# A change of order: three 1 MB weight loads leave GpSimd later in attention, and the product with the last inverse sums stands later in the output projection

## The chip, the cores and the metric

One core of a Trainium2 chip runs the whole program. The metric is the device time of one execution in microseconds (us). Three runs of the kernel before took 865.54, 867.91 and 869.71 us; the median is 867.91 us. Engines are named as in the profile: PE (TensorE's matmuls) and PEld (its weight loads), DVE (VectorE), ACT (ScalarE), POOL (GpSimd), SP (SyncE, which here only issues DMAs).

## What is computed

```python
x = x + attn(layernorm(x), qkv_w, qkv_b, proj_w, proj_b)      # x is 4 x 1024 x 256 f32
x = x + experts(layernorm(x), centroids, ln_g, ln_b, w1, b1, w2, b2)
```

Attention has 16 heads of 16 columns, rotary positions and a causal mask; its output goes through a 256 x 256 projection. Each of the 4096 tokens is then given to the one of 8 experts whose centroid has the largest product with it. The expert normalises the token, multiplies it by w1 (256 x 1024), applies relu and multiplies by w2 (1024 x 256). The result is weighted with a sigmoid of that product.

## The kernel before, in words

The kernel has three stages. Each engine has a program of its own, written out by hand; semaphores join them, and a wait holds up everything behind it on its engine.

**Projection** (to about 130 us of the span): layer norm, q, k and v. The rotated q and k are split into bf16 parts and stored to a DRAM tensor `qk_parts`.

**Attention** (about 130 to 523 us) works on 16 items Q, each being four heads of one batch; NQ is 16. An engine's `emit(i)` is one step. In step i PE computes the scores and the weighted sums of item i (`scores`, line 1252; `pv`, line 1269) and the maxima that item i+1 needs (`put_item`, line 1156). PE's first maxima product of a new item waits until that item's 14 stack transfers have landed (line 1135). ACT takes exponentials (line 929), DVE reduces block maxima (line 1009), POOL masks the diagonal blocks (line 843).

SP's order in step n (lines 735 to 757) is:

1. `store_inverse(n-3)`: wait for the reciprocals, store 16 KB (line 228).
2. `place_out(n-2)`: four transfers of 64 KB (line 213) and four of 4 KB (line 217).
3. Wait for `nm`, which POOL writes at the start of the step (lines 829 to 834), and load it in two transfers (line 744).
4. `spread_inverse(n-3)`: one transfer (line 235) that writes 4 DRAM rows of 4 KB to 64 partitions, 16 copies of each: 256 KB. Its source is broadcast as 4 x 16 x 1024.
5. `load(n+2)`: wait for PE, then the 14 stack transfers of 64 or 128 KB from `qk_parts` (lines 387 to 401).
6. In steps 5, 7 and 9, three stores of a padding row block (line 757).

POOL's order in step i: at k = 1 it writes `nm` (its first instruction is line 829, once per step); at k = 4 it issues the second weights of an expert if `early_at` names this step:

```python
        early_at = (1, 2, 3, 4, 5, 14)
        W2_AT = 4
```

Expert e's second weights (1 MB, 128 partitions of 8 KB) go to the arena columns from e times W2C. The first six experts are loaded here (LOADED is 6), and the earliest reader is the first expert product in the last stage. Even steps from 4 also hold POOL's product with the inverse sums (line 242, at k = 10). The places of the other operations are fixed by k too.

**Output projection, routing and experts** (523 us to the end). The first part has 16 pairs u of 128-token tiles. PE projects a pair (line 2053) once the addition two pairs back is done; DVE's `add(u)` (line 1673) adds the residual. Between the additions DVE has the routing: `one_hot`, `positions`, `row_scalars`, and at u = 8 `first_table`, whose end (line 1770) sets `s_tab` to 2, which names the expert and the rows of the first eight slots. POOL scatters token rows to DRAM (line 1506) group by group. The attention output of the last two items still has to be multiplied by their inverse sums; DVE does it in `normalize_out(dve, 7)`, a 128 x 1024 product (line 242) ahead of routing work, and it sets `s_nm` to 8. Who waits for that: PE before pair 12 (line 2037), and SP before it loads the second weights of expert 6 (line 1459), since the inverse sums lie in their place.

SP's order there, which is one queue: the residual rows, `col` and `b2r`, expert 6's second weights (after `s_nm`), expert 7's, then after `s_tab` the first weights of slot 0 (`load_w1`, line 246, 1 MB), then after the first four groups' scatters have landed the rows of slots 0 and 1 (line 344), then the first weights of slot 1. ACT normalises slot 0's rows (line 1557), PE turns them (line 1996) ahead of its last pair, and the experts' loop starts.

Of the kernel before, what the change touches and what calls it, by code (L numbers as in the profile page):

```python
# [130 lines left out]
def program(nc, x, x_feat, w_qkv, b_qk, b_val, w_proj, w_proj_out, b_proj, cent, w_exp, cols, b2, consts, rope, out):  # L131
    ctx = ExitStack()
    with ctx:
# [191 lines left out]
        with nc.sbuf_tensor("q_stack", [P, RS, 2, GH * SEQ], BF16) as qs, \  # L325
                nc.sbuf_tensor("k_stack", [P, RS, 2, GH * SEQ], BF16) as ks:
            s_stk = [sem(f"stack_loaded{i}") for i in range(RS)]
            s_fix = sem("fixed_rows_preset")

            phase_project_attend(nc, x, x_feat, w_qkv, b_qk, consts, rope, parts_d, w_exp, s_w, arena, v_all, spare, cst, ident, eps,  # L330
                                 qs, ks, s_fix, s_stk, s_st, s_cst, started, ones3, load_first, value_bias, add_value_bias,
                                 s_bw, load_bias_rows, split_bias, w_proj_out, ctc, xl, s_cc, centroid_means, centre_centroids, bias_columns, keep_bias_columns, bias_logits,
                                 keep_bias_logits, weight_logits, keep_weight_logits, pay_d, s_pad0, s_pad,
                                 o_late, s_vq, s_oe, s_oc, s_dc, place_out, invert_sums, store_inverse, spread_inverse, normalize_out)
# [72 lines left out]
def phase_project_attend(nc, x, x_feat, w_qkv, b_qk, consts, rope, parts_d, w_exp, s_w, arena, v_all, spare, cst, ident, eps,  # L407
# [5 lines left out]
    with ExitStack() as ctx:  # L413
# [238 lines left out]
        def wait_free(eng, i, item, alone=None):  # L652
            wait(eng, s_free, i, ITEMS, number(i, item) + 1, alone)

        early_at = (1, 2, 3, 4, 5, 14)
        W2_AT = 4
        assert len(early_at) == LOADED
        BY_POOL = NQ // 2 - 2
# [630 lines left out]
def phase_route_experts(nc, x, pay_d, load_w1, load_rows, load_half_rows, row_data, row_scalar, wait_rows, w2s, w1b, s_w1, cols, b2, cst, ident, eps, slot_tab, col, b2r,  # L1289
# [3 lines left out]
    with ExitStack() as ctx:  # L1293
# [134 lines left out]
        def expert_of(eng, S, known):  # L1428

            if S.reg is not None:  # L1430
                return expert(eng, S)
            if S.const not in known:
                known[S.const] = expert(eng, S)
            return known[S.const]
# [5 lines left out]
        with nc.Block() as block:  # L1440
# [210 lines left out]
            def _(dve):  # L1651
# [15 lines left out]
                def add(u):  # L1667
                    n, at = 2 * u + 1, 2 * u % R
                    two = xr[:, n - 1:n + 1, 0:DIM]
                    dve.wait_ge(s_pj, n + 1)  # L1670
                    last = 2 * n // G >= len(s_x) - 1
                    dve.wait_ge(s_x[-1] if last else s_x[2 * n // G], 32 if last else 16)
                    dve.tensor_tensor(two, ps_p[:, at:at + 2, 0:DIM], two, ALU.add).then_inc(s_x2, 1)
                    dve.tensor_tensor(xl[:, n - 1:n + 1, :], ps_p[:, at:at + 2, DIM:DIM + NE], xl[:, n - 1:n + 1, :],
                                      ALU.add).then_inc(s_lg, 1)

                def stats(u):
                    before = 2 * pairs_by(False, u)
                    dve.wait_ge(s_x2, u + 1)
                    if before >= R:  # L1680
                        dve.wait_ge(s_v, before + 2 - R)
                    for i in range(2):
                        dve.bn_stats(st[:, (before + i) % R, :], xr[:, 2 * u + i, 0:DIM]).then_inc(s_bn, 1)
                    for i in range(2):
                        dve.wait_ge(s_bn, before + i + 1)
                        dve.bn_aggr(mv[:, 2 * u + i, :], st[:, (before + i) % R, :]).then_inc(s_v, 1)

                def one_hot(g):
                    r, k = g % 2, GROUPS[g]
                    riota = cst[:, C_RIOTA:C_RIOTA + NE].unsqueeze(1).to_broadcast([P, k, NE])  # L1690

                    def over_experts(ap):
                        return ap.unsqueeze(2).to_broadcast([P, k, NE])

                    dve.wait_ge(s_lg, starts[g + 1] // 2)
                    dve.tensor_reduce(top[:, of(g)], xl[:, of(g), :], AX.X, ALU.max).then_inc(s_tp, 1)
                    dve.wait_ge(s_tp, 4 * g + 1)
                    dve.tensor_tensor(ge[:, 0:k, :], xl[:, of(g), :], over_experts(top[:, of(g)]), ALU.is_ge).then_inc(s_tp, 1)
                    dve.wait_ge(s_tp, 4 * g + 2)
                    dve.tensor_tensor(pick[:, 0:k, :], ge[:, 0:k, :], riota, ALU.mult).then_inc(s_tp, 1)  # L1700
                    dve.wait_ge(s_tp, 4 * g + 3)
                    dve.tensor_reduce(pm[:, 0:k], pick[:, 0:k, :], AX.X, ALU.max).then_inc(s_tp, 1)
                    dve.wait_ge(s_tp, 4 * g + 4)
                    if g >= 2:
                        dve.wait_ge(s_rk, g - 1)
                    dve.tensor_tensor(hot[:, r, 0:k, :], riota, over_experts(pm[:, 0:k]), ALU.is_equal).then_inc(s_hot, 1)

                def positions(g):
                    r, k = g % 2, GROUPS[g]
                    dve.wait_ge(s_rk, g + 1)  # L1710
                    dve.wait_ge(s_sn, g)
                    dve.tensor_tensor(rank[:, 0:k, :], ps_k[:, 0:k, :], seen[:, :].unsqueeze(1).to_broadcast([P, k, NE]),
                                      ALU.add).then_inc(s_rc, 1)
                    dve.wait_ge(s_rc, 3 * g + 1)
                    dve.tensor_tensor(seen[:, :], ps_k[:, G, :], seen[:, :], ALU.add).then_inc(s_sn, 1)
                    dve.tensor_tensor(mine[:, 0:k, :], rank[:, 0:k, :], hot[:, r, 0:k, :], ALU.mult).then_inc(s_rc, 1)
                    dve.wait_ge(s_rc, 3 * g + 2)
                    dve.tensor_reduce(posf[:, 0:k], mine[:, 0:k, :], AX.X, ALU.add).then_inc(s_rc, 1)
                    dve.wait_ge(s_rc, 3 * g + 3)
                    dve.tensor_copy(posi[:, of(g)], posf[:, 0:k]).then_inc(s_ps, 1)  # L1720

                def row_scalars(g):
                    dve.wait_ge(s_sd, 2 * (g + 1))
                    dve.reciprocal(sd[:, 2, of(g)], sd[:, 0, of(g)]).then_inc(s_rs, 1)
                    dve.reciprocal(xr[:, of(g), COL_S], sd[:, 1, of(g)]).then_inc(s_sb, 1)
                    dve.wait_ge(s_rs, g + 1)
                    dve.tensor_tensor(xr[:, of(g), COL_K], sd[:, 1, of(g)], sd[:, 2, of(g)], ALU.mult).then_inc(s_sb, 1)
                    dve.tensor_tensor(xr[:, of(g), COL_GATE], top[:, of(g)], sd[:, 2, of(g)], ALU.mult).then_inc(s_sb, 1)
                    dve.wait_ge(s_sb, 4 * g + 1)
                    dve.scalar_tensor_tensor(out=xr[:, of(g), COL_B], in0=mv[:, of(g), 0], scalar=-1.0, in1=xr[:, of(g), COL_S],  # L1730
                                             op0=ALU.mult, op1=ALU.mult).then_inc(s_sb, 1)
# [112 lines left out]
                for u in range(NP):  # L1844
                    add(u)
                    if u == 2:
                        invert_sums(dve, NQ - 1)
                    if u == 7:
                        normalize_out(dve, NQ // 2 - 1)
                    if u % 2 == 0 and 2 <= u <= 2 * FIRST_GROUPS:  # L1850
                        positions(u // 2 - 1)
                        row_scalars(u // 2 - 1)
                    if u % 2 == 1 and u < 2 * FIRST_GROUPS:
                        one_hot(u // 2)
                    if u < 2 * FIRST_GROUPS and u not in BY_ACT:
                        stats(u)
                    if u == 2 * FIRST_GROUPS:
                        first_table()
                    if u > 2 * FIRST_GROUPS:
                        stats(u - 1)  # L1860
                    if u == starts[FIRST_GROUPS + 1] // 2:
                        one_hot(FIRST_GROUPS)
                    if u in (2 * FIRST_GROUPS + 2, 2 * FIRST_GROUPS + 4):
                        dve.wait_ge(s_tab, 2)
                        expert_of(dve, Step(u // 2 - FIRST_GROUPS - 1), known)
                    if u == starts[FIRST_GROUPS + 1] // 2 + 2:
                        positions(FIRST_GROUPS)
                        row_scalars(FIRST_GROUPS)
                    if u == starts[FIRST_GROUPS + 2] // 2:
                        one_hot(FIRST_GROUPS + 1)  # L1870
# [310 lines left out]
```

## Time and profile before

| | |
|---|---|
| median of three runs | 867.91 us (865.54 to 869.71) |
| the profiled execution, own time | 862.7 us |
| its span in the profile | 861.0 us |
| mean granted clock of TensorE | 0.98 |
| PE busy in the span | 805.0 us (93%) |
| DVE, ACT, POOL busy | 594.6, 517.0, 340.4 us |

The profile shows one execution. A time in a row is counted from the start of the span. A row of the timeline names the start, the busy time, the engine, the line, the operation, the result and its inputs, and in brackets how long the engine sat idle before it and what ended that. The word "issue" there means that the engine waited for nothing that the profile shows.

### The profile page before, as it was taken

The page shows a single profiled execution, that of the slowest core. Times are in us where ns is not written, and L with a number is a line of the kernel's source. Part 1 is how long each engine was busy: PE and PEld are TensorE (multiplying, and loading weights), DVE is VectorE, ACT ScalarE, POOL GpSimd, SP SyncE. Part 2 cuts the span into 40 slices and gives each one's busy share as a digit, 9 for nine tenths or more (in the row PEclk, how much of TensorE's full clock was granted, in tenths as well). Part 3 has the DMA queues.
Part 4 walks back from the last instruction along what each step waited for, and adds up shares of the span by engine and source line. Part 5 has one row for each costly group of instructions (what it writes and reads, how often), then busy time and mean ns, then how long its engine had stood idle before and what let it go on. Part 6 is the DMA issues. An engine that isn't in the chain of part 4 may idle for free. (4 is left out here: it accounts for less than half of the span.)

```text
span 861.0 us, 24382 instructions
## 1 busy us (share of the span) xinstructions
PE 805.0 (93%) x8788; PEld 494.0 (57%) x8789; DVE 594.6 (69%) x1145; ACT 517.0 (60%) x1211; POOL 340.4 (40%) x476
## 2 busy tenths in 40 slices
PE   6999868999998999999999988877999999999994
PEld 4555433444343444443444434566999999999873
DVE  5878999999898999999999704764733333333353
ACT  4668335888787888888888894223333333333351
POOL 9999672443242434334343432634111111143211
PEclk9999988999999999999999999899999999999998
DMA  8578632445447343343334315866555555556550
GB/s 289 165 240 252 200 111 76 132 126 112 120 99 163 95 115 102 86 109 84 82 90 97 76 43 174 273 218 206 182 185 185 182 182 180 183 191 194 178 207 4
DMA packets 63354, 128.90 MB, mean 150 GB/s; under 512 B 16981, under 2 KB 44246, under 8 KB 56982
## 3 DMA queue, kind: packets, MB, share of 16 engines
q1 hardware_dynamic: 59094, 112.53, 44.5%
q0 software_dynamic: 4160, 15.03, 5.3%
q8 instruction: 64, 1.05, 0.5%
q14 instruction: 36, 0.29, 0.1%
HBM read 99.89 MB, written 22.98 MB: 143 GB/s over the span
## 5 line engine op out<-in xcount | busy, mean ns | idle before, releaser
L929 ACT ACTIVATE arena<-ps_pair 128x512 f32<-128x512 f32 (+2 forms) x640 | 317.9, 557 | 64.6 <-PE ps_pair L1252 61.8
L1009 DVE TENSOR_REDUCE B_block_max<-ps_item 128x8 f32<-128x1024 f32 x288 | 335.4, 1217 | 28.2 <-PE ps_item L1156 27.8
L1252 PE MATMUL ps_pair<-q_stack,k_stack 99*32 99x512 bf16 (+7 forms) x3072 | 197.5, 331 | 2.7 <-ACT arena L929 1.8
L843 POOL TENSOR_SCALAR_AFFINE_SELECT arena<-arena 128x256 f32<-128x256 f32 x256 | 102.1, 408 | 153.3 <-ACT arena L929 151.2
L1269 PE MATMUL ps_pair<-arena,B_v_quad 128*32 128x512 f32 (+3 forms) x1536 | 155.9, 487 | 1.2 <-ACT B_oacc L948 0.7
L1252 PEld LDWEIGHTS ps_pair<-q_stack,k_stack 99*32 99x32 bf16 (+1 forms) x3072 | 69.0, 95 | 119.7 <-ACT arena L929 60.8
L2099 PE MATMUL C_ps_p<-arena 128*128 x512 | 118.0, 382 | 4.4 <-issue 4.4
L2075 PEld LDWEIGHTS C_bank<-arena 128*128 128x128 f32 x1024 | 120.3, 193 | 2.5 <-ACT arena L1595 0.6
L2075 PE MATMUL C_bank<-arena 128*128 128x128 f32 x1024 | 120.7, 277 | 0.4 <-ACT arena L1625 0.4
L1156 PE MATMUL ps_item<-k_stack,q_stack 64*128 64x128 bf16 (+2 forms) x1280 | 107.3, 265 | 14.7 <-DVE B_block_max L1009 8.9
L1625 ACT ACTIVATE arena<-C_bank,ffn_columns 128x128 f32<-128x128 f32 x128 | 36.5, 367 | 121.9 <-PE C_bank L2075 109.8
L2099 PEld LDWEIGHTS C_ps_p<-arena 128*128 128x128 f32 x512 | 95.2, 191 | 17.6 <-issue 6.0
L1532 POOL DMA_INDIRECT out<-C_res,C_ids x32 | 31.8, 993 | 180.6 <-issue 125.8
L1156 PEld LDWEIGHTS ps_item<-k_stack,q_stack 64*128 64x128 bf16 x1280 | 45.5, 94 | 86.5 <-DVE B_block_max L1009 43.9
L1926 DVE TENSOR_SCALAR arena<-C_bank,ffn_columns 128x128 f32<-128x128 f32 x128 | 36.0, 345 | 79.0 <-PE C_bank L2075 67.2
L1269 PEld LDWEIGHTS ps_pair<-arena,B_v_quad 128*32 128x32 f32 x1536 | 42.5, 109 | 28.5 <-issue 11.5
L1196 PE MATMUL ps_pair<-arena 128*128 128x512 f32 x128 | 58.3, 598 | 0.0
L780 POOL TENSOR_TENSOR arena<-arena 128x512 f32<-128x512 f32 x32 | 51.1, 1608 | 5.6 <-DVE arena L1050 5.2
L1595 ACT ACTIVATE arena<-C_bank,ffn_columns 128x128 f32<-128x128 f32 (+1 forms) x78 | 30.8, 445 | 35.4 <-PE C_bank L1996 34.5
L1906 DVE TENSOR_TENSOR C_y<-C_ps_p,ffn_bias 128x256 f32<-128x256 f32 x32 | 13.6, 424 | 52.7 <-PE C_ps_p L2099 52.6
L1050 DVE SCALAR_TENSOR_TENSOR arena<-ps_pair,A_bq,arena 128x512 f32<-128x512 f32 x64 | 44.5, 742 | 7.6 <-PE ps_pair L1196 7.5
L1506 POOL DMA_INDIRECT payload<-C_x_rows,C_posi x32 | 31.5, 986 | 41.8 <-issue 29.3
(213 smaller groups left out, 781.0 us busy)
## 6 DMA issues: line engine op xcount, KB each, us to landing
arena<-in_w_exp SPq DMA_DIRECT2D x41, 1024.0 KB
qk_parts<-arena SPq DMA_DIRECT2D x32, 384.0 KB, 3.5
q_stack<-qk_parts SPq DMA_DIRECT2D x96, 128.0 KB, 3.5
k_stack<-qk_parts SPq DMA_DIRECT2D x64, 128.0 KB, 3.5
arena<-in_w_exp POOLq DMA_DIRECT2D x6, 1024.0 KB, 7.0
rows<-payload SPq DMA_DIRECT2D x32, 130.5 KB, 2.1
arena<-in_x SPq DMA_DIRECT2D x8, 512.0 KB, 4.7
arena<-in_x_feat SPq DMA_DIRECT2D x8, 512.0 KB, 5.6
```

The source lines that it names most:

```text
L780: pool.tensor_tensor(rot[:, h % 2, c, :], rot[:, h % 2, c, :], ds[:, h % 2, 1 - c, :], op).then_inc(s_rot, 1)
L843: pool.affine_select(out=block_p, in_=block_p, compare_op=ALU.is_ge, fill=0.0, base=0, pattern=[[0, 2], [1, P]], channel_multiplier=-1).th ...
L929: act.activation(pr[s % PR][:, h:h + 2 * n - 1:2, 0:W], ps_s[(EXPS * Q.const + exps_to[s] + u) % R][:, 0:n * W].rearrange("p (h n) -> p h ...
L1009: dve.tensor_reduce(bmx[:, g:QH:GH, first:first + 3 * gap + 1:gap], src[:, :, :].rearrange("p c (b n) -> p c b n", n=P), AX.X, ALU.max).th ...
L1050: dve.scalar_tensor_tensor(out=out[:, h % 2, at, :], in0=ps_qk[h % 2][:, c, :], scalar=bq[:, n:n + 1], in1=rp[:, table, positions(h)], op0 ...
L1156: mm = pe.matmul(dst[:, half, at * P:(at + n) * P], qs[rows, r, half, bass.ds(g * SEQ + t * P, P)], ks[rows, r, half, bass.ds(g * SEQ + kb ...
L1196: mm = pe.matmul(ps_qk[h % 2][:, c, :], wq[:, k, at:at + P], z[:, g % 2, k, :], start=(k == 0), stop=(k == DC - 1))
L1252: mm = pe.matmul(bank[at:at + 32, :], ks[rows, r, half, bass.ds(g * SEQ + kb * P + at, 32)], qs[rows, r, half, bass.ds(g * SEQ + c * QW + ...
L1269: mm = pe.matmul(ps_o[32 * h:32 * h + 32, off:QW], vq[:, r, kb, h, :], pr[s % PR][:, h, 0:QW - off], start=(kb == 0), stop=(kb == 4 * c + ...
L1625: act.activation(hr[:, S.ring(2), c, :], ps_h[0][:, c, :], ACT.Relu, bias=col[:, bass.ds(e, 1), 2 * DC + c]).then_inc(s_r[0], 1)
L2075: mm = pe.matmul(ps_h[f // HC][:, f % HC, :], w1b[:, S.ring(W1R), at:at + P], xT[:, r, c, :], start=(c == 0), stop=(c == DC - 1))
L2099: mm = pe.matmul(ps_y[r], hr[:, r, c, :], w2s[:, bass.ds(e * W2C + c * DIM, DIM)], start=(c == 0), stop=(c == FC - 1))
```

## The change

Two constants are changed. The list of steps in which the second weights are issued has 4, 6 and 8 where it had 3, 4 and 5, for experts 2, 3 and 4. The product with the last inverse sums stands behind `add(9)`, the tenth addition, where it stood behind `add(7)`; `positions(3)`, `row_scalars(3)` and `first_table` of u = 8 now stand ahead of it. No work is added or taken away.

```diff
-        early_at = (1, 2, 3, 4, 5, 14)
+        early_at = (1, 2, 4, 6, 8, 14)
...
                     add(u)
                     if u == 2:
                         invert_sums(dve, NQ - 1)
-                    if u == 7:
+                    if u == 9:
                         normalize_out(dve, NQ // 2 - 1)
```

## Rows read from the trace of the kernel before

**Rows 1.** The page: busy time of each engine in us, share of the span, instructions.

```profile
PE 805.0 (93%) x8788; PEld 494.0 (57%) x8789; DVE 594.6 (69%) x1145; ACT 517.0 (60%) x1211; POOL 340.4 (40%) x476
```

**Rows 2.** Timeline of POOL: the cast at the start of steps 3, 4, 5, 6 and 8.

```profile
199.21 0.29 POOL L829 CAST B_n<-B_nr 96x128 bf16<-96x128 f32 x1 [6.16 <-DVE B_nr L1004]
...
226.04 0.29 POOL L829 CAST B_n<-B_nr 96x128 bf16<-96x128 f32 x1 [8.32 <-DVE B_nr L1004]
...
249.94 0.29 POOL L829 CAST B_n<-B_nr 96x128 bf16<-96x128 f32 x1 [4.33 <-DVE B_nr L1004]
...
277.66 0.29 POOL L829 CAST B_n<-B_nr 96x128 bf16<-96x128 f32 x1 [8.48 <-DVE B_nr L1004]
...
325.46 0.29 POOL L829 CAST B_n<-B_nr 96x128 bf16<-96x128 f32 x1 [6.66 <-DVE B_nr L1004]
```

**Rows 3.** Timeline of all engines in steps 3 and 5: where PE stood.

```profile
215.09 0.11 PEld L1269 LDWEIGHTS ps_pair<-arena,B_v_quad 128*32 128x32 f32 x2 [1.16 <-issue]
...
222.57 0.61 PE L1156 MATMUL ps_item<-k_stack,q_stack 64*128 64x512 bf16 x4 [1.74 <-DMA k_stack<-qk_parts]
...
266.16 0.20 PEld L1156 LDWEIGHTS ps_item<-k_stack,q_stack 64*128 64x128 bf16 x6 [2.01 <-issue]
...
274.20 0.60 PE L1156 MATMUL ps_item<-k_stack,q_stack 64*128 64x512 bf16 x4 [1.94 <-DMA k_stack<-qk_parts]
```

**Rows 4.** Line 824, the weight loads: steps 3 to 5, step 4 alone, step 14 alone.

```profile
L824 POOL DMA_DIRECT2D arena<-in_w_exp x3: 591/591/593, 205.6 to 256.3; - x3
DMA to landing us min/median/max: 6.8/11.9/12.8
...
DMA to landing us min/median/max: 6.8/6.8/6.8
...
L824 POOL DMA_DIRECT2D arena<-in_w_exp x1: 591/591/591, 475.3 to 475.3; - x1
DMA to landing us min/median/max: 7.2/7.2/7.2
```

**Rows 5.** Timeline of SP's queue: the spread of the inverse sums in steps 3, 4, 5, 8, 14.

```profile
204.45 0.61 SPq L235 DMA_DIRECT2D arena<-inverse_sums  x1
...
229.52 0.59 SPq L235 DMA_DIRECT2D arena<-inverse_sums  x1
...
255.37 0.60 SPq L235 DMA_DIRECT2D arena<-inverse_sums  x1
...
330.71 0.59 SPq L235 DMA_DIRECT2D arena<-inverse_sums  x1
...
473.06 0.60 SPq L235 DMA_DIRECT2D arena<-inverse_sums  x1
```

**Rows 6.** Windows (steps 6, 7, 8, weights later): engines busy, PEclk, DMA share, GB/s.

```profile
281.66:283.66 2.00, 2.00 (x32) 0.66 (x26) 2.00 (x2) 1.64 (x4) 0.77 (x2) 1.00 0.21 59
...
311.56:313.56 2.00, 2.00 (x48) 1.22 (x44) 1.69 (x3) 1.55 (x4) 0.64 (x2) 1.00 0.81 172
...
335.46:337.46 2.00, 2.00 (x48) 1.22 (x44) 1.69 (x3) 1.55 (x4) 0.65 (x2) 1.00 0.67 195
...
553.00:566.00 13.00, 12.65 (x65) 8.69 (x66) 11.14 (x54) 1.09 (x6) 5.80 (x7) 1.00 0.91 321
```

**Rows 7.** Timeline of DVE, SP and ACT around the last product, 550 to 570 us.

```profile
550.95 1.22 DVE L242 TENSOR_TENSOR arena<-arena 128x1024 f32<-128x1024 f32 x1
...
557.29 0.67 DVE L1673 TENSOR_TENSOR C_x_rows<-C_ps_p,C_x_rows 128x512 f32<-128x512 f32 x1
...
552.20 0.80 SPq L1460 DMA_DIRECT2D arena<-in_w_exp  x2
...
558.89 0.01 SPq L246 DMA_DIRECT2D arena<-in_w_exp  x1
...
566.95 1.44 SPq L344 DMA_DIRECT2D rows<-payload  x2
...
569.05 0.60 ACT L1557 ACTIVATE arena<-rows 128x256 f32<-128x256 f32 x1 [5.01 <-DMA rows<-payload]
```

## The prediction

> **What bounds the kernel now.** I read the page first: PE is busy for 805.0 us of the span [rows 1], so a time in which PE stands still is nearly all lost. Next I looked for places where it stands. POOL's cast at the start of each attention step serves as a clock [rows 2]. From step 3 to step 4 it takes 226.04 - 199.21 = 26.83 us, from 4 to 5 23.90, from 5 to 6 27.72, and from step 6 to step 8 47.80, which is twice 23.90. So 23.90 us is an undisturbed step, and two of them are longer: step 3 by 2.93 us and step 5 by 3.82, together 6.75. The timeline says where [rows 3]. In step 3 PE's weight loads have a gap of 1.16 us that ends with "issue", and later PE waits 1.74 us for the stack of the next item: 2.90 together. In step 5 it is 2.01 and 1.94, together 3.95. The second kind is plain: the 14 stack transfers landed late. The first kind names nothing. I take it for the fetch of PE's instructions, held up on the same DMA engines; the row does not prove that.
>
> What do these two steps have? The weight loads issued in steps 3 to 5 landed 11.9, 6.8 and 12.8 us after issue, by the median, the minimum and the maximum of the three and the row of step 4 alone: 11.9 and 12.8 are steps 3 and 5 [rows 4]. Step 4 holds the same 1 MB load and the same 14 stack transfers and loses nothing. The load is therefore not enough; its neighbour on the queues matters. SP's spread of the inverse sums is issued at 204.45, 229.52 and 255.37 in these steps [rows 5]. The weight load follows the cast by 6.4 us (205.6 - 199.21 and 256.3 - 249.94 [rows 2, 4]). So the spread runs ahead of the weight load by 1.1 us in step 3, 2.9 in step 4 and 0.9 in step 5, and in step 14 by 475.3 - 473.06 = 2.2, where the load lands after 7.2 us [rows 4, 5]. The closer the spread is, the later the weight load lands.
>
> **Part one: steps 3, 4, 5 become 4, 6, 8.** The removals first. Steps 3 and 5 no longer hold a weight load. Steps 6 and 7 hold none now and take 23.90 us each, though step 7 has the three stores too [rows 2]. So both should fall to 23.90: a gain of 6.75 us. POOL's issue itself (0.59 us [rows 4]) leaves one step for another, and POOL is busy for 40% of the span [rows 1]: it costs nothing in either place. The first reader of experts 2 to 4 stands behind the whole of attention, so landing later costs nothing.
>
> The additions are steps 6 and 8; step 4 keeps a load, of another expert. Step 4 must not be priced at zero because it was clean. It was clean because PE stood 1.74 us for the stack late in step 3, when SP had already begun the next step's round, so SP was early against POOL. That stall goes. The spread of step 4 then comes about 2.9 - 1.7 = 1.2 us ahead of the weight load instead of 2.9. Step 6 loses its early start in the same way. Step 8 needs no such reasoning: its spread already stands 330.71 - 325.46 = 5.25 us behind the cast and thus 1.1 us ahead of where the weight load will be issued [rows 2, 5], exactly as in step 3. I therefore expect three crowded steps in place of two.
>
> What holds them up? While the spread has the DMA engines nearly to itself their mean share is only 0.21 [rows 6], as if few of the 16 worked on it, and a transfer has landed only when the last engine is done. The Trainium skill (DMA: Bandwidth & Descriptors, Rules for kernel authors) says that a broadcast with a leading dimension of c copies confines a DMA to at most c engines; here c is 4, a share of at most 0.25, and the trace agrees with 0.21. A weight load that meets the spread would wait on those four engines, which is why I trust the spacing more than the parity of the step.
>
> The price of one crowded step lies between 0 (step 4 now) and 3.82 us (step 5). The "issue" part was 1.16 and 2.01: I take the mean, 1.6. The stack part was 1.74 and 1.94, but in odd steps. Even steps carry their stack transfers more easily: in windows of the same kind the DMA share is 0.81 at 172 GB/s in step 7 and 0.67 at 195 GB/s in step 8 [rows 6], so the backlog should be mostly gone before the stack is needed. I take 0.4. Three steps at 2.0 make 6.0, against 6.75 lost now: part one gains 0.7 us. Its ends are a gain of 6.75 (all three like step 4 now) and a loss of 3 x 3.82 - 6.75 = 4.7.
>
> The Trainium skill (Runtime: NRT & Kernel Launch, Instruction fetch mechanics) says that the fetch of the next instruction block is mostly hidden. By that rule the "issue" part would not come back, the three steps would cost 3 x 0.4 = 1.2 and part one would gain 5.5. The gaps of 1.16 and 2.01 us in the two steps that also have late DMAs [rows 3] speak against it here.
>
> **Part two: the product behind the tenth addition.** It takes DVE 1.22 us [rows 7]. Ahead of it now come the routing of u = 8 and the first slot table, so these finish about 1.0 us earlier: the tenth addition, at 557.29 now, moves to about 556.3. What lies behind it on DVE is late by no more than 0.3. PE waits for the product only before pair 12 and has work until then, so this costs 0. POOL's scatters need the row scalars, but POOL still has an earlier group to scatter then; the gain there is 0.
>
> The cost is on SP. Its loads of experts 6 and 7 wait for this product: they go out at 552.20 now, right behind its end at 552.17, and will at 556.3 + 0.85 (the addition's two instructions) + 1.22 = 558.4. Everything behind them on SP moves too. The first weights of slot 0, at 558.89 now, follow the pair by the 0.80 us of its issue and an estimated 1.5 for reading the slot's expert: about 560.7. The rows of slot 0 are issued at 566.95, when the scatters have landed, and ACT waited 5.01 us for them until 569.05 [rows 7]. They stand third in one queue behind 3 MB of weights. Those 3 MB start 6.2 us later than the first 2 of them do now. From 553 to 566 the weights and the scatters together moved 321 GB/s [rows 6]. At that rate 3.1 million bytes take 9.8 us; with an estimated microsecond from issue to first data they end at 569.2, and about 570 with what is left of the scatters. The rows then land at about 571 instead of 569. Pair 15 and the first expert product follow the rows on PE, so I count +2.0 us. Its bounds: 0, if the weights have drained by 567, and 6.2, the whole shift.
>
> **The sum.** -0.7 + 2.0 = +1.3 us. The profiled execution took 862.7 us, 5.2 below the median of 867.91; both changes are differences, so I add the sum to the median: 869.2 us.
>
> **The rivals.**
> 1. *The crowding does not come back.* If the trouble in steps 3 and 5 was that of odd steps, 4, 6 and 8 stay at 23.90 us. For: all lost time is in odd steps, and even ones have the lighter traffic. Against: step 14 is even and its load is slower than step 4's, with nothing else new but the spacing. Part one gives -6.75; with part two at +2.0 or 0 the time is 863.2 or 861.2. Chance 0.27.
> 2. *Three full losses: slower.* The place is PE in steps 4, 6 and 8, the mechanism the same as in step 5, and it decides from about 2.9 us a step. With 3.4 us each (the mean of steps 3 and 5), 10.1 - 6.75 + 2.0 = +5.4: 873.3. For: step 8's spacing equals step 3's. Against: the lighter stack traffic. Chance 0.17.
> 3. *The fetch is hidden, the stack part stays.* -5.5 + 2.0 = -3.5: 864.4. Against: the "issue" gaps. Chance 0.08.
> 4. *My forecast*: chance 0.48.
>
> That the change does not do what it says can be set aside: both are constants that place instructions.
>
> **How the numbers follow.** A measurement of this kernel can tell about 0.5%, 4.3 us, from no change. Faster than 863.6 holds most of rival 1, a third of rival 3 and a little of my own case: 0.26. Slower than 872.2 holds most of rival 2 and the part of my own case in which part two nears its upper bound: 0.21. The rest is 0.53. The range runs from 861.7, inside rival 1, to 873.5, just over rival 2.
>
> **What the profile after would show.** Right: POOL's cast intervals of steps 3 and 5 at 23.90; those of 4, 6 and 8 at 25 to 27, with an "issue" gap on PE in each; weight loads of steps 4, 6 and 8 landing after 9 to 12 us; the spread about 1.1 us ahead of each. The pair of loads at line 1460 issued at about 558 on the clock of before, and ACT's wait at line 1557 longer by 2. Wrong: landings near 7 us in steps 6 and 8 (rival 1), or rows of slot 0 landing no later.

## The result, and the profile after

| | before | after |
|---|---|---|
| median of six runs | 866.82 us (865.54 to 869.71) | 872.63 us (871.06 to 875.45) |
| span of the profiled execution | 861.0 us | 869.4 us |

The ratio is 1.0061, with a 95% interval of 1.0036 to 1.0087: slower, by about 5.3 us. The forecast was 869.2 us, which is 1.3 over the median of three runs, 867.91; the range went to 873.5. The measured time lies inside the range, near its upper end, and the loss is about four times the forecast one. The size is that of rival 2, three full losses; the single losses are made up differently, as the rows below show. The profiled execution of the kernel before took 862.7 us, less than each of its six runs, so its trace shows less trouble than its median run has.

The page of the kernel after, first block, beside [rows 1]:

```profile
PE 808.5 (93%) x8788; PEld 495.2 (57%) x8789; DVE 597.3 (69%) x1145; ACT 517.7 (60%) x1211; POOL 338.9 (39%) x476
```

PE does the same 8788 matmuls. Its idle time has grown from 56.0 us to 60.9 (869.4 - 808.5), and its busy time by 3.5. From the cast of step 1 to that of step 15 alone, PE's busy time grew by 2.3 us (335.13 to 337.46) for the same 5392 matmuls, which needs a reason of its own (below). The timeline of POOL shows which steps grew longer; it is the clock of [rows 2], here from step 4 on:

```profile
224.16 0.29 POOL L829 CAST B_n<-B_nr 96x128 bf16<-96x128 f32 x1 [6.65 <-DVE B_nr L1004]
252.51 0.29 POOL L829 CAST B_n<-B_nr 96x128 bf16<-96x128 f32 x1 [5.85 <-DVE B_nr L1004]
276.40 0.29 POOL L829 CAST B_n<-B_nr 96x128 bf16<-96x128 f32 x1 [6.65 <-DVE B_nr L1004]
303.14 0.29 POOL L829 CAST B_n<-B_nr 96x128 bf16<-96x128 f32 x1 [5.13 <-DVE B_nr L1004]
327.04 0.29 POOL L829 CAST B_n<-B_nr 96x128 bf16<-96x128 f32 x1 [6.65 <-DVE B_nr L1004]
356.04 0.29 POOL L829 CAST B_n<-B_nr 96x128 bf16<-96x128 f32 x1 [9.42 <-DVE B_nr L1004]
```

Step 4 takes 28.35 us, step 6 26.74 and step 8 29.00; steps 5 and 7 take 23.9. Over 23.90 that is 4.45, 2.84 and 5.10, together 12.4, where [rows 2] had 6.75. From the cast of step 1 to that of step 15 the kernel before took 341.41 us and the kernel after 347.20: 5.8 us more. From the cast of step 15 to the end it is 369.77 against 368.22, 1.55 more. The remaining 1.06 us of the 8.4 between the two spans lie ahead of step 1, where nothing was changed.

Where PE stood, from the timeline of PE in steps 4, 6 and 8, beside [rows 3]:

```profile
241.44 0.24 PE L1252 MATMUL ps_pair<-q_stack,k_stack 128*32 128x128 bf16 x3 [2.52 <-issue]
...
292.36 0.23 PE L1156 MATMUL ps_item<-k_stack,q_stack 64*128 64x128 bf16 x2 [1.89 <-issue]
...
299.68 0.61 PE L1156 MATMUL ps_item<-k_stack,q_stack 64*128 64x512 bf16 x4 [0.93 <-DMA k_stack<-qk_parts]
...
351.18 0.61 PE L1156 MATMUL ps_item<-k_stack,q_stack 64*128 64x512 bf16 x4 [3.74 <-DMA k_stack<-qk_parts]
```

These are the two kinds of gap of [rows 3], in another mixture in each step: step 4 has only the gap with "issue", step 8 only the wait for the stack, step 6 both. The gaps of steps 4 and 8 do not fill their losses: 2.52 of 4.45 and 3.74 of 5.10 us. The windows right behind them tell what else there is (the kernel after, columns as in [rows 6]):

```profile
238.90:241.40 2.50, 0.02 (x1) 0.00 (x0) 1.77 (x2) 0.19 (x1) 0.59 (x2) 1.00 1.03 198
241.40:244.00 2.60, 2.56 (x35) 0.90 (x35) 0.33 (x1) 1.26 (x3) 1.03 (x3) 0.81 1.03 203
244.00:248.00 4.00, 4.00 (x56) 1.55 (x52) 2.77 (x3) 2.59 (x5) 2.66 (x2) 0.70 0.38 83
...
351.20:353.00 1.80, 1.80 (x20) 0.52 (x24) 1.38 (x2) 0.83 (x2) 0.00 (x0) 0.79 0.48 78
353.00:356.00 3.00, 3.00 (x23) 0.66 (x15) 1.60 (x3) 1.49 (x4) 0.00 (x0) 0.56 0.03 4
```

PE is busy again, but part of the time at the lower of its two clock levels (1.2 in place of 2.4 GHz). In step 4 that loses 2.6 x 0.19 + 4 x 0.30 = 1.7 us, in step 8 1.8 x 0.21 + 3 x 0.44 = 1.7 us. With it the gaps account for the losses: 2.52 + 1.7 = 4.2 of 4.45 us in step 4, 1.89 + 0.93 = 2.8 of 2.84 in step 6, and 3.74 + 1.7 = 5.4 in step 8, which is 5.10 over and its successor 0.19. Behind the stack wait of step 5 before, which was 1.94 us, the clock stayed at 1.00:

```profile
274.20:276.00 1.80, 1.80 (x20) 0.58 (x24) 1.37 (x2) 0.81 (x2) 0.00 (x0) 1.00 0.67 117
```

The weight loads of these three steps (line 824) and the spread ahead of each (line 235, timeline of SP), beside [rows 4, 5]:

```profile
L824 POOL DMA_DIRECT2D arena<-in_w_exp x1: 593/593/593, 230.5 to 230.5; - x1
DMA to landing us min/median/max: 11.3/11.3/11.3
...
L824 POOL DMA_DIRECT2D arena<-in_w_exp x1: 593/593/593, 282.8 to 282.8; - x1
DMA to landing us min/median/max: 11.5/11.5/11.5
...
L824 POOL DMA_DIRECT2D arena<-in_w_exp x1: 593/593/593, 333.4 to 333.4; - x1
DMA to landing us min/median/max: 11.5/11.5/11.5
```

```profile
229.72 0.59 SPq L235 DMA_DIRECT2D arena<-inverse_sums  x1
...
281.48 0.59 SPq L235 DMA_DIRECT2D arena<-inverse_sums  x1
...
332.46 0.59 SPq L235 DMA_DIRECT2D arena<-inverse_sums  x1
```

The spread is 0.8, 1.3 and 0.95 us ahead. The place of the trouble and its neighbours on the queues came as the prediction had them, and the landings within its 9 to 12 us. Its size did not: the prediction had these steps at 25 to 27 us and an "issue" gap in each, and step 8 has none.

The second part of the change, from the timelines of DVE, SP and ACT, beside [rows 7]:

```profile
564.80 1.22 DVE L242 TENSOR_TENSOR arena<-arena 128x1024 f32<-128x1024 f32 x1
...
566.05 1.84 SPq L1460 DMA_DIRECT2D arena<-in_w_exp  x2
...
574.68 1.44 SPq L344 DMA_DIRECT2D rows<-payload  x2
...
577.76 1.09 ACT L1557 ACTIVATE arena<-rows 128x256 f32<-128x256 f32 x2 [3.71 <-DMA rows<-payload]
```

Counted from the cast of step 15 (499.63 here, 492.78 before), the loads of experts 6 and 7 leave SP at 66.4 in place of 59.4 us, and ACT has the rows of slot 0 at 78.1 in place of 76.3, 1.9 us later. Half of that is the rows' own issue, which the prediction held fixed: it comes at 75.1 in place of 74.2. From issue to ACT's start it is 3.1 us in place of 2.1. The first expert product on PE follows at 83.6 in place of 83.0.

### The profile page after: what moved, and what is told of

It reads as the page before. It is cut to its first block and busy times, and to the rows that moved or that the text cites. A ratio compares the mean times of both kernels' runs of the same rounds, so it can differ in the third digit from the quotient of the medians.

```text
span 869.4 us, 24382 instructions
## 1 busy us (share of the span) xinstructions
PE 808.5 (93%) x8788; PEld 495.2 (57%) x8789; DVE 597.3 (69%) x1145; ACT 517.7 (60%) x1211; POOL 338.9 (39%) x476
## 3 DMA queue, kind: packets, MB, share of 16 engines
q8 instruction: 64, 1.05, 0.5%
## 5 line engine op out<-in xcount | busy, mean ns | idle before, releaser
L2099 PE MATMUL C_ps_p<-arena 128*128 x512 | 119.8, 384 | 3.2 <-issue 2.9
L780 POOL TENSOR_TENSOR arena<-arena 128x512 f32<-128x512 f32 x32 | 49.1, 1546 | 4.4 <-DVE arena L1050 4.0
```

Of the source, the lines that this page charges most:

```text
L780: pool.tensor_tensor(rot[:, h % 2, c, :], rot[:, h % 2, c, :], ds[:, h % 2, 1 - c, :], op).then_inc(s_rot, 1)
L2099: mm = pe.matmul(ps_y[r], hr[:, r, c, :], w2s[:, bass.ds(e * W2C + c * DIM, DIM)], start=(c == 0), stop=(c == FC - 1))
```

## The experiments

None of the twelve kernels leaves out work. Each ratio is to the kernel before, run beside it on the same chip. k is the place within POOL's step at which the load is issued. "Lost" is the time from the cast of step 1 to that of step 15 in the one profiled execution, less 14 x 23.90 us; by this count the kernel before lost 6.8 and the kernel after 12.6. It comes from one execution, and the ratio from the medians.

| kernel | weights in steps, k | spread | lost | ratio (95%) |
|---|---|---|---|---|
| weights only | 1, 2, 4, 6, 8, 14; k = 4 | narrow | 18.2 | 1.0071 (1.0047 to 1.0095) |
| product only | as before | narrow | 7.4 | 1.0009 (0.9992 to 1.0027) |
| wide spread | as before | wide | 1.1 | 0.9908 (0.9883 to 0.9934) |
| moved, wide | 1, 2, 4, 6, 8, 14; k = 4 | wide | 0.2 | 0.9911 (0.9881 to 0.9941) |
| four narrow pieces | as before | narrow x4 | 9.7 | 0.9998 (0.9980 to 1.0017) |
| late | 1, 2, 14, 14, 15, 15 | narrow | 0.1 | 0.9898 (0.9873 to 0.9923) |
| late and wide | 1, 2, 14, 14, 15, 15 | wide | 0.1 | 0.9910 (0.9885 to 0.9935) |
| k = 6 | 1, 2, 4, 6, 8, 14; k = 6 | narrow | 10.7 | 1.0022 (0.9996 to 1.0049) |
| k = 2 | 1, 2, 4, 6, 8, 14; k = 2 | narrow | 0.4 | 0.9911 (0.9884 to 0.9938) |
| spread last | 1, 2, 4, 6, 8, 14; k = 4 | narrow, last | 2.4 | 0.9926 (0.9898 to 0.9955) |
| whole change, k = 2 | 1, 2, 4, 6, 8, 14; k = 2 | narrow | 0.0 | 0.9919 (0.9891 to 0.9947) |
| k = 2 again | 1, 2, 4, 6, 8, 14; k = 2 | narrow | 0.0 | 0.9903 (0.9873 to 0.9934) |

**1. The weight loads alone.**

```diff
-        early_at = (1, 2, 3, 4, 5, 14)
+        early_at = (1, 2, 4, 6, 8, 14)
```

> Half of the change: the list of steps is (1, 2, 4, 6, 8, 14), the product stays behind the eighth addition. In the trace of the changed kernel the cast intervals of steps 4, 6 and 8 are 28.35, 26.74 and 29.00 us (4.45, 2.84 and 5.10 over 23.90), together 12.4 us against the 6.75 that steps 3 and 5 lost before. Theory A (the loss is the crowding of the weight load and the spread in each step that has both close together): the same three intervals again, 26.5 to 29, steps 3, 5 and 7 at 23.9; the time 4 to 6 us over the kernel before. Rival B (the loss has to do with the moved product, or was chance in one execution): steps 4, 6 and 8 at 24 to 25 and the time within 1 us of the kernel before.

Measured: 862.20 us (858.23 to 866.75) against 856.12, which is +6.1. Steps 4, 6 and 8 took 31.35, 28.90 and 28.89 us; the landings were 14.0, 12.0 and 11.3 us, with the spread 0.5, 1.65 and 1.05 ahead. Theory A holds; step 4 and the time came out above its upper ends, 29 us and +6. The profiled execution was the slowest of the nine runs (866.75), so 18.2 us lost is more than the median run has. The PE waits of attention (the table of waits: total, times, longest):

```profile
PE ps_item L1156 <- DMA k_stack<-qk_parts: 8.5, 4, 3.5
PE ps_pair L1252 <- issue: 2.6, 1, 2.6
PE ps_item L1156 <- issue: 2.1, 1, 2.1
```

The stack is 8.5 of it, in even steps. So the parity of the step protects nothing.

**2. The product alone.**

```diff
-                    if u == 7:
+                    if u == 9:
                         normalize_out(dve, NQ // 2 - 1)
```

> The other half: the weight loads stay in steps (1, 2, 3, 4, 5, 14), the product goes behind the tenth addition. By the prediction's second part the loads of experts 6 and 7 leave SP about 6.2 us later, the rows of slot 0 land 2 us later and the kernel takes 2.0 us more (bounds 0 to 6.2). In the two traces the stretch from the cast of step 15 to the end is 369.77 us against 368.22, so 1.5 us more. Theory A: +1 to +2.5 us, and ACT's wait for the rows of slot 0 ends 1.5 to 3 us later counted from the cast of step 15. Rival: the later rows only eat waiting that exists anyway behind them, 0 to +0.5 us. Attention: steps 3 and 5 at 26.8 and 27.7 us as in the kernel before.

Measured: 856.73 us against 856.12, +0.8 us by the ratio, -0.7 to +2.3. Counted from the cast of step 15, SP's pair of loads went at 61.5 us, 5.0 later than in experiment 1, which has the product in its old place; ACT had the rows at 74.6 against 74.3. The first link of the prediction's chain is there, but here the rows came only 0.3 us later. That speaks for the rival; the time, with its interval, allows both. The loss in attention is that of the kernel before, 7.4 us, so what the change loses there comes from experiment 1.

**3. The wide spread.**

```diff
-            sp.dma_start(inv_all[half:half + HALF, :],
-                         inv_d[Q].unsqueeze(1).to_broadcast([QH, HD, SEQ])).then_inc(s_rb, 16)
+            for h in range(QH):
+                sp.dma_start(inv_all[half + h * HD:half + (h + 1) * HD, :],
+                             inv_d[Q][h:h + 1, :].to_broadcast([HD, SEQ])).then_inc(s_rb, 16)
...
-            eng.wait_ge(s_rb, 32 * (pair + 1))
+            eng.wait_ge(s_rb, 128 * (pair + 1))
```

> The kernel before with the spread of the inverse sums issued as four transfers, one for each head, whose leading dimension is the 16 copies and no longer the 4 heads. The same bytes go to the same places. Theory A (the spread sits on about four of the 16 DMA engines, and a weight load that meets it there lands late and holds up the stack and PE): the DMA share right behind the spread rises from 0.21 to over 0.5, the weight loads of steps 3 and 5 land in 7 to 9 us in place of 11.9 and 12.8, the intervals of steps 3 and 5 fall from 26.8 and 27.7 to 24 to 25, and the time falls by 3 to 6.5 us, less whatever SP's 1.8 us of further issue time in each step costs. Rival B (the whole load on the DMA engines, not its placing on few of them, sets the loss): the loads still land after 11 to 13 us, steps 3 and 5 stay at 26.5 to 28, the time is the same or up to 2 us longer.

Measured: 848.05 us against 856.12, -7.9 us (-10.0 to -5.7), more than the 3 to 6.5 expected. The weight loads of steps 3 to 5 landed after 5.5, 6.3 and 6.5 us. The casts of steps 3 to 6, timeline of POOL (its line is 830 here):

```profile
199.02 0.29 POOL L830 CAST B_n<-B_nr 96x128 bf16<-96x128 f32 x1 [6.15 <-DVE B_nr L1005]
222.91 0.29 POOL L830 CAST B_n<-B_nr 96x128 bf16<-96x128 f32 x1 [6.65 <-DVE B_nr L1005]
247.34 0.29 POOL L830 CAST B_n<-B_nr 96x128 bf16<-96x128 f32 x1 [4.34 <-DVE B_nr L1005]
271.76 0.29 POOL L830 CAST B_n<-B_nr 96x128 bf16<-96x128 f32 x1 [6.66 <-DVE B_nr L1005]
```

Step 3 takes 23.89 us; steps 4 and 5 take 24.43 and 24.42. The windows right behind the spread of steps 6 and 8, columns as in [rows 6]:

```profile
277.60:279.60 2.00, 2.00 (x50) 0.96 (x42) 1.59 (x3) 1.35 (x4) 0.82 (x2) 1.00 0.65 131
...
325.50:327.50 2.00, 2.00 (x50) 0.93 (x45) 1.59 (x3) 1.35 (x4) 0.90 (x3) 1.00 0.57 137
```

The DMA share is 0.65 and 0.57, where it was 0.21 [rows 6], for the same 256 KB. The Trainium skill (DMA: Bandwidth & Descriptors, Rules for kernel authors) ties the number of engines to the outermost dimension, and copies in front are its example. The prediction took c for the copies; here the 4 in front are the heads, and the 16 copies stand behind them. The trace agrees with the rule, with 4 in front at 0.21 and 16 in front at 0.6. Theory A holds.

**4. The change's list with the wide spread**: the edits of experiments 1 and 3 together.

> The change's list of steps (1, 2, 4, 6, 8, 14) together with the spread in four transfers of 16 leading copies, as in the run before it with that spread. There steps 3 and 5 fell to 23.89 and 24.42 us and the weight loads landed after 5.5 to 6.5 us. Theory A (the change loses because the narrow spread is close ahead of three weight loads): the intervals of steps 4, 6 and 8 at 23.9 to 24.5 us instead of 31.35, 28.90 and 28.89, landings of 5.5 to 7, time 6 to 9 us under the kernel before. Rival B (the wide spread only helped in odd steps): steps 4, 6, 8 above 26 us.

Measured: 848.55 us against 855.94. Steps 4, 6 and 8 took 24.11, 23.89 and 23.91 us, the loads landed after 6.0, 5.6 and 7.7. One edit to the spread takes all of the change's loss away, in even steps as in odd ones.

**5. The control: four issues, but narrow** (the count for `s_rb` as in experiment 3).

```diff
+            for k in range(QH):
+                m = SEQ // QH
+                sp.dma_start(inv_all[half:half + HALF, k * m:(k + 1) * m],
+                             inv_d[Q][:, k * m:(k + 1) * m].unsqueeze(1).to_broadcast([QH, HD, m])).then_inc(s_rb, 16)
```

> A control for the wide spread: the kernel before with the spread issued as four transfers too, but cut by columns, so that each still leads with the 4 heads. SP has the same four issues, and the stack transfers leave it as much later as with the wide spread. Theory A (only the number of engines counts): the DMA share behind the spread stays at about 0.2, the weight loads of steps 3 and 5 land after 10 to 14 us, these steps stay at 26.5 to 28.5 us, the time is within 3 us of the kernel before. Rival C (the four issues help, because they delay the stack transfers by 1.2 us): steps 3 and 5 near 24 us, time 5 to 8 us less.

Measured: 855.36 us against 855.94, the same time. The share behind the spread of step 6 stays low, in a window as before:

```profile
285.80:287.80 2.00, 2.00 (x30) 0.67 (x26) 2.00 (x3) 1.68 (x5) 0.82 (x2) 1.00 0.21 73
```

Steps 3 and 5 took 29.70 and 26.82 us, with landings of 11.5 and 9.4, where 26.5 to 28.5 and 10 to 14 were expected. The profiled execution was the second slowest of ten (860.25), so its 9.7 us lost is more than the median run has. Four issues, and the delay that they bring, gave no gain; a leading dimension of 16 did. All of PE's waits over 0.2 us are for the stack here (5.9 us in three waits), and none ends with "issue". Behind the longest, 3.65 us in step 3, the granted clock is at its lower level:

```profile
224.80:226.50 1.70, 1.67 (x12) 0.46 (x16) 1.02 (x1) 0.04 (x1) 0.00 (x0) 0.50 0.55 94
226.50:230.00 3.50, 3.50 (x25) 0.78 (x17) 1.52 (x3) 2.02 (x4) 0.00 (x0) 0.50 0.06 9
```

**6. The loads late.**

```diff
-        early_at = (1, 2, 3, 4, 5, 14)
+        early_at = (1, 2, 14, 14, 15, 15)
```

> The kernel before with the weight loads of experts 2 to 5 in steps 14, 14, 15 and 15, two in each: steps that have a spread but no stack transfers. Theory A (a step is lost by spread, weight load and stack transfers together): no attention step is longer than 24.2 us up to step 13; in steps 14 and 15 no wait for the stack can occur, and only gaps that end with issue may, 0 to 2 us each; the time 3 to 6.5 us under the kernel before. Rival C (the spread and the weights alone hold up PE's instructions, the stack has no part): steps 14 and 15 lose 2 to 4 us each, and the time is within 2 us of the kernel before.

Measured: 847.55 us (846.79 to 848.76) against 856.12, -8.7 us (-10.9 to -6.6), more than expected. Every step is at 23.9 us. The loads still landed late, after 8.0 to 12.6 us, but PE waited for no transfer there. Spread and weights together cost nothing here without the stack behind them. This run and experiment 3 also price the crowding in the kernel before: 8 to 9 us by the medians, more than the 6.8 of its one profile.

**7. Both remedies**: the edits of experiments 3 and 6.

> Both remedies: the wide spread and the second weights of experts 2 to 5 in steps 14, 14, 15 and 15. Each alone brought attention to 23.90 us a step but for 0.5 us in two steps, and took 8.1 and 8.6 us off. Theory A (they remove the same loss): no further gain, 8 to 9.5 us under the kernel before. Rival (each also removes something of its own): 11 us or more under it.

Measured: 847.56 us against 855.94, as each alone. They remove the same loss. The loads of steps 14 and 15 now landed after 5.2 to 7.2 us.

**8. The loads two places later in the step.**

```diff
-        early_at = (1, 2, 3, 4, 5, 14)
-        W2_AT = 4
+        early_at = (1, 2, 4, 6, 8, 14)
+        W2_AT = 6
```

> The change's list of steps with the narrow spread as it was, but each weight load two places later in its step (k = 6 for k = 4), about 3.3 us later. The spread is then some 4.4 us ahead of the weight load in place of 0.5 to 1.7, more than the 2.9 and 3.3 us at which step 4 stayed at 23.90 and 24.41. Theory A (the distance decides): landings near 7 us, steps 4, 6 and 8 at 23.9 to 24.5, time 6 to 8 us under the kernel before. Rival B (the 1 MB and the stack in one step are too much, wherever in it): since the weights now lie on top of the stack transfers, the stack comes as late or later: 26 to 30 us in each of the three steps.

Measured: 858.16 us against 855.94. This is a miss for theory A: the spread was 3.6, 4.2 and 3.9 us ahead, yet two of the loads landed after 12.1 and 11.5 us (the third after 6.7), and steps 4, 6 and 8 took 28.51, 26.23 and 24.73. Steps 1 and 2, which have no spread at all, took 25.17 and 25.52 where they had 23.9. The waits of PE in attention:

```profile
PE ps_item L1156 <- DMA k_stack<-qk_parts: 9.5, 5, 3.1
```

No wait ends with "issue". So the two kinds of gap come apart. A load that lies on top of the stack transfers delays the stack, with a spread ahead or without. The "issue" gap was seen only where the load stood close behind the narrow spread. The distance to the spread alone, on which the prediction rested, is not the rule.

**9. The loads two places earlier** (`W2_AT = 2`, with the change's list).

> The change's list of steps, the narrow spread as it was, and each weight load two places earlier in its step (k = 2 for k = 4): about 3.6 us after the cast, 1 to 2 us ahead of the spread, and all 3.3 us further from the stack transfers. Theory A2 (two parts: a weight load that finds the narrow spread ahead of it ends late and holds up what PE fetches; one that still lies under the stack transfers delays the stack): the weights are ahead of the spread and have about 5.5 to 7 us of the engines before the stack matters, so landings of 5.5 to 7.5, steps 4, 6 and 8 at 23.9 to 25, time 5 to 8 us under the kernel before. Rival B (any meeting of the two, whichever goes first, costs the same): 26 us and more in each.

Measured: 860.04 us against 867.04, -7.7 us. The casts of steps 4 to 7:

```profile
225.09 0.29 POOL L829 CAST B_n<-B_nr 96x128 bf16<-96x128 f32 x1 [6.66 <-DVE B_nr L1004]
249.00 0.29 POOL L829 CAST B_n<-B_nr 96x128 bf16<-96x128 f32 x1 [4.33 <-DVE B_nr L1004]
273.25 0.29 POOL L829 CAST B_n<-B_nr 96x128 bf16<-96x128 f32 x1 [7.01 <-DVE B_nr L1004]
297.15 0.29 POOL L829 CAST B_n<-B_nr 96x128 bf16<-96x128 f32 x1 [4.33 <-DVE B_nr L1004]
```

The loads went 4.7, 3.2 and 4.2 us ahead of the spread (226.31, 274.48, 322.27 against 231.01, 277.68, 326.52), since they were issued 1.2 us after the cast and not 3.6 as expected, and landed after 5.3 to 5.4 us. PE waited once for the stack, 0.5 us. The load is now ahead of the spread, but also 5 us further from the stack transfers; this run does not tell which of the two helps. The next one leaves the load in its place.

**10. The spread last in SP's round.**

```diff
-                    if n.const >= 3:
-                        spread_inverse(sp, n.const - 3)
                     Q = n + 2
                     if Q.within(NQ):
                         load(Q)
+                    if n.const >= 3:
+                        spread_inverse(sp, n.const - 3)
```

> The change's list of steps, weight loads at k = 4, and in SP's round the narrow spread stands behind the 14 stack transfers of the round instead of ahead of them. Theory A2: the weight load now meets only the stack transfers, as in steps 1 and 2, which took 23.9 us each; landings of 5.5 to 8 in steps 4, 6 and 8, these steps at 23.9 to 25, no gap of PE that ends with issue over 1 us, time 5 to 8 us under the kernel before. Rival D (the spread then sits on top of the last stack transfers and the stack lands as late as before): a wait for the stack of 1 to 3 us in those steps and perhaps in all steps from 3 on, time at or above that of the kernel before.

Measured: 860.89 us against 867.04, -6.4 us. The loads landed after 6.2, 5.7 and 6.5 us, and PE never waited for the stack. Instead POOL's cast came late after the even steps from 4 on, which hold its product with the inverse sums (steps of 28.31, then 20.34 us): the product now waits for the later spread, and twice PE waited for `nm` behind it, 1.9 us in all. Theory A2 holds, at a small price that it did not name; and with a late cast, a single interval of this clock says nothing.

**11. The whole change with k = 2**, and **12. its partner without the second part**, on one chip.

> The whole change (steps 1, 2, 4, 6, 8, 14 and the product behind the tenth addition) with the weight loads at k = 2 in place of k = 4. With the change's list alone and k = 2 the kernel took 0.9911 of the kernel before, about 7.7 us less. Theory A (the second part costs next to nothing: alone it measured 1.0009): within 1.5 us of the run beside it, that is 0.989 to 0.994 of the kernel before. Rival (the second part costs the 2.0 us of the prediction, hidden before by the noise): 2 us more than the run beside it, 0.993 or 0.994. Attention steps of 23.9 us in both.

> The kernel with the change's list and k = 2 again, with the product at its old place, as the partner of the run beside it on the same chip: 0.989 to 0.993 of the kernel before, all attention steps at 23.9 to 24.3 us. If it came out at 0.995 or more, the first measurement of it was luck.

Measured: 861.54 and 859.75 us, against 868.47. All steps are at 23.9 in both. The rows of slot 0 (timeline of ACT), the whole change first, then its partner:

```profile
566.77 1.09 ACT L1557 ACTIVATE arena<-rows 128x256 f32<-128x256 f32 x2 [4.49 <-DMA rows<-payload]
```

```profile
565.79 0.60 ACT L1557 ACTIVATE arena<-rows 128x256 f32<-128x256 f32 x1 [5.51 <-DMA rows<-payload]
```

Counted from the cast of step 15 (486.37 and 487.51) that is 80.4 and 78.3: 2.1 us later. The first expert product is 1.5 us later, yet from the cast to the end it is 371.63 and 371.59 us. The medians differ by 1.8, the ratios' intervals overlap. Of the 2.1 us, 1.0 is the rows' own later issue (77.25 in place of 76.23). Between 0 and 2 us the second part's price stays open.

## Why the prediction was wrong in size and right in place

**Which engine and which steps: right.** The loss is PE's idle time in steps 4, 6 and 8; steps 3, 5 and 7 fell to 23.9 us. That step 4 was clean before only through SP's early start was right too: the spread came 0.8 us ahead of the load (1.2 forecast), and the step lost 4.45 us.

**The neighbour: right, and shown.** Widening the spread, moving the load ahead of it, moving the spread behind the stack or moving the loads away from the stack each took the loss away; four narrow pieces did not. The sign by which the prediction told a crowded step, the distance to the spread alone, failed in experiment 8: a load that meets the stack is enough. That only few engines carry the spread was read from one window, and the windows of experiments 3 and 5 show it.

**The price of a crowded step: wrong, the term that failed.** The prediction took 1.6 us for "issue" and 0.4 for the stack, 2.0 a step. Measured were 4.45, 2.84 and 5.10, a mean of 4.1. The "issue" part held as a mean over the three steps, (2.52 + 1.89 + 0) / 3 = 1.5, though not as one gap in each. (The 1.16 and 2.01 us of [rows 3] are idle times of PEld; by its own timeline PE stood 0.25 and 1.79 us there.) What failed is the stack's 0.4: PE waited 0, 0.93 and 3.74 us for it, a mean of 1.6, and 8.5 us over four waits in experiment 1. And a term was missing: in steps 4 and 8 the granted clock fell behind the gap, which cost 1.7 us each, 1.1 a step as a mean, and stood in no row of attention before. 1.5 + 1.6 + 1.1 is 4.2. The reason given was that even steps carry lighter stack traffic, from the DMA shares of two windows in steps without a weight load [rows 6]. Such a window tells how the stack flows by itself, not how it flows behind a load that ends 5 us late. The mean of the two stalls that the trace did show (3.4 us, rival 2) was the better price. With 4.1, part one is 12.4 - 6.75 = +5.6, against -0.7 in the prediction.

**The fetch.** The Trainium skill (Runtime: NRT & Kernel Launch, Instruction fetch mechanics) calls the fetch mostly hidden, which would have had the "issue" part gone; the trace differs, if the gaps are the fetch, with 2.52 and 1.89 us in steps 4 and 6. They were seen only in steps with the load close behind the narrow spread (before, after, experiments 1 and 2), though not in each, and in none of experiments 3 to 12. The traces say more than the prediction used. They list transfers of 16 KB on a DMA queue of the kind "instruction". This is the window 238.3:238.5 of the kernel after, ahead of the gap that ends at 241.44:

```profile
q8 instruction: 1, 0.02, 47.8%
```

47.8% of 16 engines' 0.2 us is 1.5 us, so this transfer ended at about 239.9 and PE went on 1.5 us later. Each of the seven gaps (1.16 us of PEld, 1.68 to 2.56 us of PE) ended 1.4 to 1.7 us after the end of such a transfer. And they stand at fixed places of PE's program: in step 4 ahead of the last three of four matmuls of line 1252 both in the kernel after and in experiment 1. That makes it very likely that PE waits for its own instructions there; no run changed the fetch alone.

**Part two: the chain half right, its end open.** SP's loads left 7.0 us later (6.2 forecast) and the rows came 1.9 later (2.0 forecast). That these two agree is partly luck: 0.9 of the 1.9 is the rows' later issue, which the prediction had unchanged, and its microsecond from issue to first data and its 1.5 us for reading the slot's expert were guesses that no row gave. The bracket of ACT's wait did not grow by 2 us as forecast but fell from 5.01 to 3.71, since ACT came to it later. What reached the end was 1.55 us in the two profiles, +0.8 (-0.7 to +2.3) by itself, and in experiments 11 and 12 0.0 by the profiles and 1.8 by the medians.

**The sum.** Forecast -0.7 + 2.0 = +1.3; by the profiles 5.8 + 1.55 = +7.3 and 1.06 of chance ahead of step 1; by the medians +5.8. The range held the result because it had been drawn to just over rival 2, not because the sum was near. The chance of 0.17 for rival 2 looks too low: the spacing of step 8, which the prediction itself found equal to step 3's, was its best evidence, and a mean of seen stalls had been set aside for a softer argument.

## What to carry to other kernels

A DMA whose outermost dimension was 4 kept the DMA share at 0.21, and in steps with stack transfers a 1 MB load issued 0.5 to 1.7 us behind it landed after 9.4 to 14.0 us; away from it, and from the stack transfers, it took 5.3 to 7.9. So look for a low DMA share at a time when a transfer is under way, and put a dimension of 16 or more in front. When a stall in the trace is to be moved, take its own size as the price of the next one, add what the clock costs behind it, and check both its causes in the new place. Here it was the moment within the step that was wrong, not the list of steps: with `W2_AT = 2` or the wide spread the same list of steps gives 0.990 to 0.992 of the kernel before, and the loads in steps 14 and 15 give 0.9898.

## What the runs showed of the hardware beyond this

**A gap can cost more than its length.** Behind or within each of PE's five gaps of 2.95 us and more (3.74 in the kernel after, 2.95 and 3.54 in experiment 1, 3.65 in experiment 5, 3.10 in experiment 8) the granted clock fell to 0.50 and stayed there for 3.4 us, in experiment 5 for 6.8; 3.4 us at half the clock cost a busy PE 1.7. Shorter gaps went either way. Behind those of 1.68 to 2.09 us in the kernels before and after and in experiment 2, and behind one of 2.44 in experiment 8, it stayed at 1.00. Of two of 2.5 us it fell behind one (kernel after) and not behind the other (experiment 1). And it fell behind one of 1.81 us in experiment 1, which another of 2.14 preceded by 8 us, and behind one of 1.93 in experiment 5:

```profile
306.40:309.80 3.40, 3.40 (x27) 0.67 (x16) 1.96 (x5) 2.18 (x5) 0.40 (x2) 0.53 0.27 42
```

```profile
278.80:282.10 3.30, 3.30 (x27) 0.69 (x19) 1.87 (x4) 2.13 (x5) 0.29 (x1) 0.51 0.28 47
```

So the length of a gap alone does not tell whether the clock falls, and what else decides stays open. In experiment 1 the gaps (13.0 us) and three such stretches (5.1 us) make 18.1 of the 18.2 us lost.

**A kernel with crowding scatters.** In the runs on one chip the kernels without lost steps spread over 2.0 us (846.79 to 848.76, experiment 6) and 3.0 us (846.88 to 849.83, experiment 3), those with them over 8.5 (experiment 1) and 10.3 us (experiment 8); these had 9 and 10 runs, those 6 each. The stalls differ from execution to execution, so one profile gives their kind, not their mean.

**The level depends on the chip.** The kernel before took 855.9 and 856.1 us on one chip, on two occasions, and 866.8, 867.0 and 868.5 on others. From the cast of step 15 on the profiles differ mainly in one place, the start of the experts' loop. Windows of the kernel before and of experiment 1 there, columns as in [rows 6]:

```profile
592.00:596.00 4.00, 2.07 (x9) 1.22 (x9) 0.00 (x0) 0.00 (x0) 2.99 (x4) 1.00 0.42 146
596.00:600.00 4.00, 1.87 (x6) 1.04 (x6) 0.00 (x0) 0.00 (x0) 1.96 (x2) 1.00 0.28 100
```

```profile
605.00:609.00 4.00, 4.00 (x28) 3.72 (x27) 2.09 (x12) 0.61 (x2) 3.08 (x4) 1.00 0.90 222
```

In the first, PE is busy for half of 8 us at full granted clock, with short gaps that end with "issue", and ACT and DVE do nothing; in the second it is busy throughout. From the cast of step 15 to the end the slower chips take 368 to 372 us, the faster one 357 to 361. No transfer of the kind "instruction" falls between 590 and 602 us in the first, so these gaps are not the fetch of the attention steps. What causes them stays open; it is in both kernels and no part of the change. Only kernels run on the same chip can be compared.
